# The third attention's queries: the first experts' rows added to the residual by accumulating transfers from GpSimd

## The reference

```python
x = x + xattn0(layernorm(x), ctx, ctx, mask)            # 16 heads of 16 values
x = x + ffn0(layernorm(x))                              # its own attention, a norm, 4 experts (one each token), a norm
x = x + xattn1(layernorm(x), ctx, ctx, side, side, pad, attn_mask)
x = x + ffn1(layernorm(x))                              # 16 experts (two each token) and 2 shared ones
```

## Time and profile before

| | |
|---|---|
| median of 3 runs | 1687.59 us (1684.16 to 1690.16) |
| the profiled execution's own time | 1687.02 us |
| its span, first to last instruction | 1685.2 us |
| VectorE's first add of `queries` | 880.55 us after the start of the span |
| GpSimd's first bias of `queries` starts | 913.49 us |
| the next stage's first score matmul | 919.02 us |

### The profile page before, as it was taken

How to read it: one execution, slowest core, us unless ns; L and a number is a source line. 1 busy time by engine, 2 the same in 40 slices (tenths; PEclk the granted TensorE clock), 3 DMA queues, 4 the chain that set the end, 5 groups by cost and what they waited for, 6 DMA issues and landing times. The chain is left out here.

```text
span 1685.2 us, 24349 instructions
## 1 busy us (share of the span) xinstructions
PE 1527.7 (91%) x8288; PEld 1021.2 (61%) x8288; DVE 1069.6 (63%) x2656; ACT 838.9 (50%) x1341; POOL 530.2 (31%) x348
## 2 busy tenths in 40 slices
PE   7899999979999997779956799899989999999996
PEld 4566666665654545469954555555554666677774
DVE  5699999854887776636646888888766450222221
ACT  3688888725566672312215777777632222111110
POOL 0112110003000000401113999999613226133323
PEclk9999999989999999889987999999999999999999
DMA  7433422106343314367737888988441002244541
GB/s 255 163 126 112 131 89 64 38 14 225 95 113 107 100 54 157 136 235 249 254 120 266 293 302 294 301 299 297 152 167 59 1 13 97 74 139 144 141 145 12
DMA packets 135558, 254.02 MB, mean 151 GB/s; under 512 B 29723, under 2 KB 67504, under 8 KB 126096
## 3 DMA queue, kind: packets, MB, share of 16 engines
q1 hardware_dynamic: 124256, 241.11, 43.2%
q0 software_dynamic: 10128, 10.35, 2.3%
q10 hardware_dynamic: 1056, 1.05, 0.2%
HBM read 202.69 MB, written 54.39 MB: 153 GB/s over the span
## 5 line engine op out<-in xcount | busy, mean ns | idle before, releaser
L667 DVE CUSTOM_DVE_ANT_0 X<-pS,M 128x512 f32<-128x512 f32 x512 | 340.7, 689 | 58.8 <-POOL M L594 37.8
L617 PE MATMUL pT<-ident,X 128*128 128x128 f32 x2048 | 305.6, 272 | 2.8 <-ACT PT L705 2.8
L608 PE MATMUL pS<-k,q 65*128 65x512 f32 (+1 forms) x512 | 254.4, 497 | 44.8 <-DVE mx L667 31.6
L594 POOL TENSOR_TENSOR M<-C,M 128x2048 f32<-128x2048 f32 x63 | 286.0, 4584 | 4.8 <-DMA M<-in_fside_Bx16xSxS 4.4
L617 PEld LDWEIGHTS pT<-ident,X 128*128 128x128 f32 x2048 | 254.1, 140 | 42.4 <-issue 4.9
L608 PEld LDWEIGHTS pS<-k,q 65*128 65x128 f32 (+1 forms) x512 | 98.1, 192 | 163.4 <-DVE mx L667 99.9
L468 PE MATMUL pO<-PT,V 128*17 128x512 f32 x1536 | 194.6, 597 | 0.0
L865 DVE TENSOR_REDUCE nm<-pS 128x1 fp32r<-128x512 f32 x256 | 161.2, 684 | 39.1 <-PE pS L838 28.7
L695 ACT ACTIVATE X<-X,nm 128x512 f32<-128x512 f32 x256 | 164.1, 712 | 24.9 <-POOL nm L576 24.6
L695 ACT ACTIVATE X<-X,mx 128x512 f32<-128x512 f32 x256 | 165.1, 715 | 3.6 <-DVE mx L667 3.1
L679 DVE COPY PT<-pT 128x1024 f32<-128x1024 f32 x128 | 156.1, 1220 | 6.7 <-PE pT L617 6.7
(11 more groups left out here) (321 smaller groups left out, 2251.7 us busy)
## 6 DMA issues: line engine op xcount, KB each, us to landing
M<-in_fside_Bx16xSxS SPq DMA_DIRECT2D x64, 1024.0 KB, 7.1
w<-in_L_ffn_ew SPq DMA_DIRECT2D x48, 512.0 KB, 5.3
w<-in_L_ffn_W SPq DMA_DIRECT2D x23, 1024.0 KB, 5.4
q<-q_stacks SPq DMA_DIRECT2D x192, 64.0 KB, 3.6
k<-k_stacks SPq DMA_DIRECT2D x128, 64.0 KB, 3.0
k_stacks<-hi SPq DMA_DIRECT2D x24, 256.0 KB, 2.3
q_stacks<-hi SPq DMA_DIRECT2D x24, 256.0 KB, 2.1
q_stacks<-lo SPq DMA_DIRECT2D x24, 256.0 KB, 2.0
```

Of the source, the lines that this page charges most:

```text
L594: eng.tensor_tensor(M[:, slot], C[:, b % 2], M[:, slot], ALU.subtract).then_inc(s_m, 1)
L608: eng.matmul(pS[:, qt % 2, :], of, by, start=True, stop=True).then_inc(s_s, 1)
L617: ins = eng.transpose(pT[:, kt, qt * P:(qt + 1) * P], X[:, t % 3, qt, kt * P:(kt + 1) * P], self.ident[:])
L667: eng.tensor_tensor_reduce(X[:, i % 3, qt, :], pS[:, qt % 2, :], M[:, slot, qt, :], 2.0 if not per_group else 1.0, HIGHEST if not per_grou ...
```

## The change

The tile `y` and the semaphore `s_a` go. GpSimd issues the four loads first thing in the stage, straight into `x`, with an addition at the destination. SyncE, which issued them before, now waits for the second of them to have landed before it goes on to `C`, `M` and the keys. VectorE's 16 additions go. Its other work and the rest of the stage stay as they are.

```diff
-            y = self.sb("y", [P, NT, D], ctx=ctx)
...
                 @block.sync
                 def _(eng):
-                    for b in range(B):
-                        eng.dma_start(y[:, b * ST:(b + 1) * ST, :], YS[b * S:(b + 1) * S].rearrange("(t p) d -> p t d", p=P)).then_inc(s_g[b], 16)
+                    eng.wait_ge(s_g[1], 16)
                     eng.dma_start(self.C[:, 0], common[0]).then_inc(self.s_c[0], 16)
...
                 @block.gpsimd
                 def _(eng):
+                    for b in range(B):
+                        eng.dma_start(x[:, b * ST:(b + 1) * ST, :], YS[b * S:(b + 1) * S].rearrange("(t p) d -> p t d", p=P),
+                                      accum_op=ALU.add).then_inc(s_g[b], 16)
                     eng.memset(self.q2[AUX:P, :, 0, :].bitcast(F32), 0.0).then_inc(s_zero, 1)
...
                         eng.wait_ge(s_g[b], 16)
                         for n in rows:
-                            eng.tensor_tensor(x[:, n, :], x[:, n, :], y[:, n, :], ALU.add).then_inc(s_a, 1)
-                        for n in rows:
-                            eng.wait_ge(s_a, n + 1)
                             eng.bn_stats(st[:, n, :], x[:, n, :]).then_inc(s_st, 1)
```

More of the change, by code:

```diff
@@ L1422, in queries @@
             pj = self.ps("pj", [P, 4, 512], ctx)
-            names = ("s_a", "s_st", "s_ag", "s_var", "s_dev", "s_rs", "s_z", "s_tr", "s_ev", "s_p", "s_sc", "s_t", "s_hi", "s_lo")
-            s_a, s_st, s_ag, s_var, s_dev, s_rs, s_z, s_tr, s_ev, s_p, s_sc, s_t, s_hi, s_lo = (self.sem(n, ctx) for n in names)
+            names = ("s_st", "s_ag", "s_var", "s_dev", "s_rs", "s_z", "s_tr", "s_ev", "s_p", "s_sc", "s_t", "s_hi", "s_lo")
+            s_st, s_ag, s_var, s_dev, s_rs, s_z, s_tr, s_ev, s_p, s_sc, s_t, s_hi, s_lo = (self.sem(n, ctx) for n in names)
             s_g = [self.sem("s_g", ctx) for _ in range(B)]
```

## The result

The changed kernel takes 1692.36 us (median of 13 runs, 1688.42 to 1694.55), the kernel before in runs beside it 1688.77 (1684.16 to 1693.23). The ratio is 1.002, with an interval of 1.0012 to 1.0029: slower by 3.6 us. The interval leaves out 1, but the size lies within the 0.3% that the prediction counts as no change. 1698.5 was forecast. The profiled execution took 1690.27 us with a span of 1688.3, so 3.1 us more span than before.

A forecast was written before the change was run, and what follows sets the result against it. No engine is full; a chain of waits up to VectorE's last low part sets the end. That part 8.9 us later plus 2.0 of clock, on 1687.02, gives 1697.9, stated as 1698.5 for the median; 8-in-10 range 1687.5 to 1707.

The forecast's parts named there:

- the sum: End of the stage: last low part 8.9 us later plus 2.0 us of clock, 10.9 us slower in all.
- the first packets of `C` come 1.2 us later: In SyncE's queue: after its wait ends at 887.5, the first bytes of `C` move at 888.7.
- L2 and L3: Times at which batches 2 and 3 have landed, put at 895.4 and 906.5; no change needs below 892.9 and 897.6.
- The 8.9 us term: In the query stage: VectorE's last low part ends at 922.2 instead of 913.34, since batch 3 lands late.
- the 2.0 us of clock: TensorE waits for batch 3, its clock falls low, turn 3 and project 2 slow down: up to 3.3 us, 2.0 taken.
- The turns: Transfer engines take one packet from each queue in turn, so an adding row beside `C` and `M` costs 0.415 us.
- the prediction's worse case: Engines take several packets of `C` a turn: batch 2 waits until 903, and the end is 1.5 us later still.
- rival 2: Engines serve the adding queue first or delay it little: 1688.6, or 1686.5 with GpSimd at its lower bound; chance 0.33.
- GpSimd's issue: Time a direct transfer of 512 rows keeps GpSimd busy: 3.1 us taken, bounds 0.96 and 6.2.
- z1: End of batch 1's `z` on VectorE: forecast at 891.6, 1.0 us later than before.
- The term costed at nothing: SyncE's queue behind its wait: `C`, first `M` and first `hi` are wanted only later, so the delay was called covered.
- Adds of batches 2 and 3: VectorE's additions for these batches lie beside ScalarE's work, so removing them was called worth nothing.

The follow-up runs named there:

- their control: The kernel before with eight buffers instead of four for the high and low query parts; ratio to the kernel before 0.9998, stage 36.91 us.

## Why the prediction was off

- **Direction and bounds.** Slower, as forecast, with the result inside the range of 1687.5 to 1707, but by 3.6 us instead of 10.9, and by another mechanism than the sum's. The direction is luck: the path that was to make it did not occur, and a wait that the prediction did not have made it. Its own sign of being wrong came true, a `bn_stats` of batch 3 before 898.
- **The step that failed** is "the first packets of `C` come 1.2 us later". The 1.2 us came from `y`, which starts on idle engines. Behind a busy adding queue it was 4.0 us (885.49 to 889.5, and again 4 us with `C` after batch 0). By 889.5 batch 2 was through, and all but 130 packets of batch 3, so hardly a turn was left to pay. L2 and L3 were put at 895.4 and 906.5; the batches were there by 890.18 and 894.03 at the latest, under both limits (892.9 and 897.6). The 8.9 us term is gone, and with it the 2.0 us of clock: TensorE's granted clock stays at 1.00 from 895 to 910. The run with `C` after batch 0 is the test: the same silence, ending 2.6 us sooner after the start of the stage, and both terms are back (10.0 us of stage).
- **The turns** were right in kind and near in size: 0.376, 0.376 and 0.41 us a row, for 0.415, in the three runs where two full queues met. The rule of round robin by packets (the Trainium skill, "DMA: Bandwidth & Descriptors", "Queues, rings and completion order") agrees with 427 packets beside 426; several packets of `C` for one adding row, the prediction's worse case, are ruled out by these counts. Once both queues move, neither is served first, as rival 2 had it. Rival 2's outcome (under both limits, 1686.5 to 1688.6) came by another road, and its time too was missed: it had 1.0 us of loss at most, and 3.6 were measured. The chance of 0.33 for the ground up to 1692.6 covers the result.
- **GpSimd's issue** was taken as 3.1 us and measured 5.34 / 4 = 1.3, near the lower bound of 0.96. The rule of the Trainium skill ("DMA: Bandwidth & Descriptors", anatomy of a GpSimd transfer) that many descriptors can be emitted before more cost shows agrees: four times the rows of a plain scatter for 1.3 us instead of 0.96. With 0.083 us a row (2.7 us a batch; the 196 GB/s end of the estimate) the first `bn_stats` began at 882.85 instead of 884.2. z1 came at 13.6 us after the start against 13.9 before, where 1.0 us of loss was predicted. The 2.7 us of adds were spent on later landing, nearly to the last.
- **The term costed at nothing.** Behind SyncE's wait the prediction looked at when `C`, `M` and the first `hi` are wanted, and found cover for each. It did not ask when the *first four slots* are wanted again. The fifth cast wants its slot 6.9 us after the first low part is issued (898.45 to 904.62 + 0.69), so a landing later than that shows. That is the 1.98 us, shown by the two runs with eight slots and their control. It was at no place in the sum.
- **Adds of batches 2 and 3** worth nothing: right within 0.2 us, shown with two batches left to VectorE.
- **The rest of 3.6 us.** In the profiles the stage is 1.4 us longer. The gap behind the first bias grows by 0.33 us (last row of the first fence; 0.34 us before). The next stage, from second bias to its end, took 334.0 us before, 335.0 and 334.8 in two profiles of the changed kernel, and 333.1 and 335.3 in two with eight slots, so it wanders by 1 us on its own. Of the 3.6 us, 1.7 are shown; the interval of the ratio allows 2 to 5. What lies between stays open.

## What to carry to other kernels

When a wait is put ahead of a queue, list every later transfer in it, down to the small ones, and ask for each not only who reads it but whose buffer it frees: with four slots for eight parts a landing that comes 5 us later became a wait, with eight it did not. Loads that add took twice the engine time of plain ones here and lost most when they ran beside a queue of large packets (7.5 to 11.4 us of stage), so a price of turns has to be multiplied by the packets that really meet. When they meet decides: issue times 2.8 us apart made the difference between 3.6 and 8.7 us.

## What was unexpected in the hardware

- A queue that is issued while the other is busy stays silent for about 4 us, then shares one to one. For `C` behind adding rows it was 3.7 to 4.3 us in six profiles (885.49 to 889.5 and 882.94 to 887.1 among them), whether 130 or 689 packets were left; on idle engines its first packets came after 0.9 us in three (876.89 to 877.8, 885.20 to 886.1, 888.97 to 889.9). The other way round, adding rows issued at 877.38 beside a busy q1 had no packet up to 882.5; in the changed kernel, on idle engines, they ran within some 2 us. What sets the 4 us was not tried.
- SyncE's four issues of `M` took 4.01 us instead of 1.91 while the adding queue was full, and 2.16 with `C` after batch 3.
- Each direct transfer of GpSimd in the stage goes with 0.08 us more between the first bias and the next stage's: the gap is 0.34 us without any, 0.42 with one, 0.50 with two, 0.67 with four, in all profiles but the one in which `M` was late. Why was not tried.
